# An eight-stage transformer kernel on one core: bias rows added on VectorE, and the memory layer prepared in four blocks

## The reference

```python
x = x + _L0_attn_ref(_layernorm(x), ...)   # 16 heads, softmax
x = x + _L0_ffn_ref(_layernorm(x), ...)    # gelu(x w1 + b1) w2 + b2, 512 hidden
x = x + _L1_attn_ref(_layernorm(x), ...)   # 16 heads of 64
x = x + _L1_ffn_ref(_layernorm(x), ...)
x = x + _L2_attn_ref(_layernorm(x), ...)   # 16 heads over three neighbouring tokens
x = x + _L2_ffn_ref(_layernorm(x), ...)    # 8 experts, the best one
x = x + _L3_attn_ref(_layernorm(x), ...)   # a memory that learns, below
x = x + _L3_ffn_ref(_layernorm(x), ...)    # 8 experts, the best two, and a shared one
```

```python
k, v, q = (causal_dwconv(hidden @ W.T, cw, cb) for k, v, q)          # 4 taps
alpha = (sigmoid(hidden @ aW.T + ab) * 0.1).mean(-1)
eta   = (sigmoid(hidden @ eW.T + eb) * 0.9 + 0.05).mean(-1)
theta = (softplus(hidden @ tW.T + tb) * LR).mean(-1)
# of each chunk: g = clipped gradient of |W2 silu(W1 k) - v|^2 at the chunk's first weights, then
S = eta * S - theta * g ;  W = (1 - alpha) * W + S                  # token by token
out = W2_t silu(W1_t q) ; out = rms_norm(out @ Wo.T) * norm_g * (hidden @ gW.T + gb)
```

## Time and profile before

| what | value |
|---|---|
| time, median of 3 runs | 3157.16 us (3152.45 to 3158.06) |
| profiled execution: its time, its span | 3151.58 us, 3149.8 us |
| PE busy, its weight loads | 2954.1 us (94%), 1838.4 us |
| DVE, ACT, POOL busy | 2210.3, 1419.3, 734.6 us |
| PE clock granted, mean | 0.91 of full speed |

### The profile page before, as it was taken

The page is one execution under the profiler, slowest core; times in us unless marked ns, Lnnn a source line. Parts: engine busy times, 40 slices in busy tenths (PEclk is TensorE's granted clock), DMA queues, the critical chain, the costliest instruction groups (busy, mean ns, idle before and its releaser), DMA issues. The chain is left out here.

```text
span 3149.8 us, 43331 instructions
## 1 busy us (share of the span) xinstructions
PE 2954.1 (94%) x15864; PEld 1838.4 (58%) x15864; DVE 2210.3 (70%) x4583; ACT 1419.3 (45%) x2681; POOL 734.6 (23%) x608
## 2 busy tenths in 40 slices
PE   4999999999987999999999999999999787789799
PEld 2666666666654555555555555555554444556587
DVE  5788888888724877777877777777774637777554
ACT  1666666666641344444444444444444210322343
POOL 1000000000000244444444444444444100055200
PEclk7999999999987899999999999999999867555598
DMA  4112122121004011111111111111100100000000
GB/s 96 26 26 51 29 49 45 33 51 21 1 8 121 1 41 41 41 41 31 38 27 28 41 41 41 41 38 31 35 20 1 37 1 9 3 1 2 16 1 14
DMA packets 42128, 95.91 MB, mean 30 GB/s; under 512 B 12502, under 2 KB 31676, under 8 KB 32188
## 3 DMA queue, kind: packets, MB, share of 16 engines
q1 hardware_dynamic: 41916, 93.14, 13.0%
HBM read 35.18 MB, written 7.34 MB: 13 GB/s over the span
## 5 line engine op out<-in xcount | busy, mean ns | idle before, releaser
L957 ACT ACTIVATE l1a_PT<-l1a_st 128x512 f32<-128x512 f32 x1024 | 597.1, 598 | 759.6 <-PE l1a_st L873 755.5
L974 DVE TENSOR_REDUCE l1a_m<-l1a_aux 128x1 f32<-128x512 f32 x1024 | 667.6, 685 | 125.3 <-PE l1a_aux L835 123.1
L478 DVE TENSOR_REDUCE l0s_mquad<-l0s_mx 128x1 f32<-128x512 f32 x1024 | 635.5, 684 | 169.3 <-PE l0s_mx L346 169.3
L924 POOL TENSOR_TENSOR l1a_acc<-l1a_acc,l1a_PT 128x1024 f32<-128x1024 f32 x224 | 570.0, 2545 | 680.5 <-ACT l1a_PT L957 680.5
L454 ACT ACTIVATE l0s_PT<-l0s_st 128x512 f32<-128x512 f32 x1024 | 529.2, 601 | 236.0 <-PE l0s_st L362 232.6
L886 PE MATMUL l1a_ov<-l1a_PT,l1a_V 128*64 128x512 f32 x2048 | 495.7, 605 | 0.0
L871 PE MATMUL l1a_st<-l1a_QA,l1a_KA 128*128 128x512 f32 x1024 | 447.1, 437 | 2.4 <-issue 2.3
L362 PE MATMUL l0s_st<-l_QS,l_KS 128*128 128x512 f32 x1024 | 437.4, 430 | 3.6 <-ACT l0s_PT L454 3.5
L346 PE MATMUL l0s_mx<-l_KS,l_QS 120*128 120x512 f32 x1024 | 415.9, 412 | 20.4 <-DMA l_KS<-qk_rows 20.4
L873 PE MATMUL l1a_st<-l1a_QB,l1a_KB 65*128 65x512 f32 x1024 | 405.6, 396 | 0.0
L835 PE MATMUL l1a_aux<-l1a_KA,l1a_QA 128*128 128x512 f32 x1024 | 398.5, 437 | 0.8 <-DVE l1a_lo L986 0.8
(11 more groups left out here) (348 smaller groups left out, 2763.7 us busy)
## 6 DMA issues: line engine op xcount, KB each, us to landing
l1a_KA<-l1a_hi SPq DMA_DIRECT2D x32, 512.0 KB, 7.9
l_QS<-qk_rows SPq DMA_DIRECT2D x64, 192.0 KB
l_KS<-qk_rows SPq DMA_DIRECT2D x64, 192.0 KB
l1a_QA<-l1a_hi SPq DMA_DIRECT2D x16, 512.0 KB, 4.5
l1a_QA<-l1a_lo SPq DMA_DIRECT2D x16, 512.0 KB, 8.6
l1a_QB<-l1a_hi SPq DMA_DIRECT2D x16, 512.0 KB, 4.5
l1a_KB<-l1a_lo SPq DMA_DIRECT2D x16, 512.0 KB, 6.4
...
```

What stands on the lines that cost most here:

```text
L478: nc.vector.tensor_reduce(mquad[:, u % 2, tile, g:g + 1], mx[:, n % MX0, :], axis=AX.X, op=ALU.max).then_inc(mx_free[n % MX0], 1)
L924: nc.gpsimd.tensor_tensor(acc[:, h % 2, 1, :], first, PT[:, g % PT_SLOTS, :], ALU.add).then_inc(added_pool, 1)
L957: nc.scalar.activation(PT[:, g % PT_SLOTS, (u % 2) * CW:(u % 2 + 1) * CW], st[:, u % ST1, :], ACT.Exp, scale=1.0 / float(np.sqrt(HD1))).th ...
L974: nc.vector.tensor_reduce(m4[:, b, q, c:c + 1], src, axis=AX.X, op=ALU.max).then_inc(aux_read, 1)
```

## The change

1. The bias rows go. `bv`, `bo`, `b2`, `sb2` and `gb` are loaded as 128 equal rows. In four stages DVE adds the bias to `X` at the stage's start (`add_bias`). V and the gate get it as DVE takes them out of PSUM; for V this moves ACT's copies to DVE, and PE's wait for V is now one for the PSUM buffer (`mx_free`).
2. In `l3_ffn`, the four products of mask and expert biases of a block move from the end into the loop, as one more `down` in groups 7, 9, 11 and 13.
3. `l3_prepare` works in four blocks of 512 tokens. ACT folds tanh, the first tap and abs differently; E runs on 128 partitions (two copies of 32 rows and one of 64), and C and A are one scan beside each other, so that two scans stand for three. The initial values of the multipliers come from POOL, which writes `d1` (128x2048), the zero columns and, later, the squared keys. Key-query products are made two chunks at a time.
4. `l3_scan` scales keys (`ktc`, two ACT operations) and queries (`qa`, two POOL operations) chunk by chunk.
5. Semaphores of early stages are cleared for reuse by POOL at the start of L1's feed-forward.

```diff
+def add_bias(nc, X, bias, biased):
+    for c in range(NC):
+        x = X[:, TPC * c:TPC * (c + 1), :]
+        nc.vector.tensor_tensor(x, x, bias[:, :].unsqueeze(1).broadcast_to([P, TPC, D]), ALU.add).then_inc(biased, 1)
...
-                        nc.tensor.matmul(o[:, t * D:(t + 1) * D], xnT[:, at], Wt[:, 2, :], start=True, stop=False)
-                        last = nc.tensor.matmul(o[:, t * D:(t + 1) * D], ones[0:1, 0:P], bv[0:1, :],
-                                                start=False, stop=True)
+                        last = nc.tensor.matmul(o[:, t * D:(t + 1) * D], xnT[:, at], Wt[:, 2, :], start=True, stop=True)
...
-                nc.tensor.matmul(o, vT[:, t * P:(t + 1) * P], Wo[:, :], start=True, stop=False)
-                nc.tensor.matmul(o, ones[0:1, 0:P], bo[0:1, :], start=False, stop=True).then_inc(done, 1)
+                nc.tensor.matmul(o, vT[:, t * P:(t + 1) * P], Wo[:, :], start=True, stop=True).then_inc(done, 1)
...
+            dve.wait_ge(loaded.sem, loaded.all)
+            add_bias(nc, X, bo, biased)
             for c in range(NC):
+                dve.wait_ge(biased, c + 1)
                 dve.wait_ge(done, TPC * (c + 1))
...
-                        nc.tensor.matmul(o, ones[0:1, 0:P], b2[0:1, :], start=True, stop=False)
                         for b in range(NB):
...
+            if g - 1 in TURNED_AT:
+                mine.append((N3, TURNED_AT.index(g - 1)))
...
-                pe.wait_ge(mt_read, NC)
-                for c in range(NC):
-                    biases(c)
...
+            def sums(c):
+                pe.wait_ge(tanh_done, c + 1)
...
+            project(0)
+            project(1)
+            sums(0)
+            project(2)
+            sums(1)
+            project(3)
+            sums(2)
+            sums(3)
             pe.wait_ge(gain_done, 2)
+            gate(0)
+            gate(1)
+            turn()
             for c in range(NC):
+                key_query(c)
+            gate(2)
+            gate(3)
...
+            def conv(c):
+                dve.wait_ge(raw_done, c + 1)
+                dve.wait_ge(y_done, c + 1)
...
+                nc.vector.tensor_tensor_scan(T["E"][:, cols(c)], eta[:, cols(c)], d1[:, cols(c)], 0.0, ALU.mult, ALU.add
+                                             ).then_inc(e_done, 1)
+                dve.wait_ge(e_done, c + 1)
+                nc.vector.tensor_tensor_scan(T["C"][:, cols(c)], oma[:, cols(c)], T["E"][:, cols(c)], 0.0,
+                                             ALU.mult, ALU.add).then_inc(c_done, 1)
...
-                    nc.tensor.matmul(y1, state[:, o % 4, 0, 0, :], T["qA"][:, at(o)], start=True, stop=False)
+                    nc.tensor.matmul(y1, state[:, o % 4, 0, 0, :], qa[:, o % 2, 0, :], start=True, stop=False)
...
+                    for i, th in enumerate((thC, thE)):
+                        nc.scalar.activation(ktc[:, c % 2, i, :], T["ktok"][:, c, :], ACT.Copy, scale=th[:, c:c + 1]
+                                             ).then_inc(s["ktc_done"], 1)
...
+                    for i, coef in enumerate((T["A"], T["C"])):
+                        nc.gpsimd.tensor_tensor(qa[:, c % 2, i, :], T["q"][:, at(c)], coef[0:DM, at(c)], ALU.mult
+                                                ).then_inc(s["qa_done"], 1)
...
-            for kt, th in ((ktokC, thC), (ktokE, thE)):
-                link.open(nc.vector.tensor_tensor(kt[:, :, :], T["ktok"][:, :, :],
-                                                  th[:, :].unsqueeze(2).broadcast_to([CHUNK, NCH, DM]), ALU.mult))
```

More of the change, by code:

```diff
@@ L1780, in _ @@
                     add(d, *downs[d])
-                for c in range(NC):
-                    add(len(downs) + c, N3, c)
 DM = 32
@@ new lines, in gate, with turn @@
+            def gate(i):
+                b = GATE_BANK[i]
+                pe.wait_ge(oma_done, 2 * (b + 1))
+                if b == 0:
+                    pe.wait_ge(kt_read, 2)
+                for t in range(TPC):
+                    n = TPC * i + t
+                    last = nc.tensor.matmul(pp[:, b, t * D:(t + 1) * D], xnT[:, n * P:(n + 1) * P], gW[:, :],
+                                            start=True, stop=True)
+                last.then_inc(gate_full, 1)
+            def turn():
+                pe.wait_ge(conv_done, NC)
+                for n in range(NT):
+                    last = nc.tensor.transpose(pp[:, 0, n * DM:(n + 1) * DM], T["k"][0:DM, n * P:(n + 1) * P],
+                                               ident[0:DM, 0:DM])
+                last.then_inc(kt_full, 1)
@@ new lines, in key_query @@
+            def key_query(c):
+                pe.wait_ge(eta_done, 2 * (c + 1))
+                pe.wait_ge(q_done, c + 1)
+                for n in range(TPC * c, TPC * (c + 1)):
+                    at = slice(n * P, (n + 1) * P)
+                    last = nc.tensor.matmul(pb[:, c, (n % TPC) * P:(n % TPC + 1) * P], T["k"][0:DM, at], T["q"][:, at],
+                                            start=True, stop=True)
+                last.then_inc(kq_full, 1)
+            project(0)
+            project(1)
@@ L1934, in _ @@
+            gate(2)
+            gate(3)
+            pe.wait_ge(ln_done, 1)
+            pe.wait_ge(gate_read, 1)
+            for n in range(NT):
+                last = nc.tensor.matmul(pp[:, 1, n:n + 1], soft[MAIN, n * P:(n + 1) * P], lead[MAIN, 1:2],
+                                        start=True, stop=True)
+            last.then_inc(th_full, 1)
         @block.scalar
         def _(act):
-            link = Chain(act, act_order)
             act.wait_ge(loaded.sem, loaded.all)
-            link(nc.scalar.activation(raw[:, 0:TAPS - 1], cw[:, 0:TAPS - 1], ACT.Copy, scale=0.0))
@@ new lines, in _ @@
+            project(0)
+            project(1)
+            act.wait_ge(d1_set, 1)
+            eta_of(0)
+            project(2)
+            eta_of(1)
+            project(3)
+            eta_of(2)
+            eta_of(3)
+            for c in range(NC - 1):
+                query(c)
+            move(0)
+            for c in range(NC - 1):
+                value(c)
+            query(NC - 1)
+            act.wait_ge(half_set, 1)
+            act.wait_ge(abs_done, NC)
+            nc.scalar.activation(soft[3 * DM:4 * DM, :], tn[low, :], ACT.Ln, scale=0.5, bias=half[low, :]).then_inc(ln_done, 1)
@@ new lines, in _ @@
+            dve.wait_ge(raw_set, 1)
+            conv(0)
+            conv(1)
+            dve.wait_ge(starts_set, 2)
+            dve.wait_ge(d1_set, 1)
+            scans(0)
+            conv(2)
+            scans(1)
+            conv(3)
+            scans(2)
+            dve.wait_ge(gain_done, 2)
+            gate(0)
+            scans(3)
+            gate(1)
+            for c in range(NC):
+                key_query(c)
+            gate(2)
+            gate(3)
+            dve.wait_ge(ksq_done, 1)
```

438 lines of the change are left out of this document (219 added, 219 removed).

## The result

The changed kernel takes 3076.82 us (median of 4 runs, 3072.86 to 3079.14) against 3154.80 (median of 4, 3147.02 to 3158.06); the ratio is 0.9755, 95% interval 0.9732 to 0.9778. It is 78 us faster; the forecast of 3072 was 4.8 us too low.

What follows compares the result with a forecast made beforehand. PE was taken to bound most attention and feed-forward stages, DVE `l3_prepare`, a ring of small steps the scan. Terms summed to -81.9 us: 3069.7 from the profiled execution, 3075.3 from the median, forecast 3072; 8-in-10 range 3057 to 3091.

Steps and rivals of the forecast that it cites:

- Surcharge of height: PE, alternating product heights: each product costs about 0.27 us (slow clock) or 0.19 (fast) more; removing bias products returns it.
- L0 attention and output: V products and output projection of L0 without bias products: -10.7 us and -10.3 us.
- L0 feed-forward: L0's feed-forward, PE-bound: 16 tiles at -0.63 us each without bias products, -10.1 us.
- L2 attention: L2's output projection: four blocks, each dropping from 5.79 to 1.79 us on the path, -16.0 us.
- Last feed-forward: End of the last feed-forward: -11.4 us at the end, +5.1 for mask products returning in four groups, -6.3 us.
- Preparation: `l3_prepare`, bound by DVE: 32.6 us of work, 4.3 of waits including 1.6 for theta's products; -32.3 us.
- Scan's start: Start of the L3 scan: two DVE operations go and ACT's table load comes ahead, -2.3 us.
- Scan: L3 scan: DVE operations starting right after POOL ones lengthen, 0.19 us per chunk for 31 chunks, +5.8 us.
- Only the bias product's own time goes: Rival, bias stages: remaining tall products stay at 0.72 or 0.40 us, together 15.7 us dearer, 3088; 12%.
- Blocks don't overlap: Rival, `l3_prepare`: each block's chain runs alone, so -10 us instead of -32, 3094; 6%.
- POOL blocks DVE: Rival, scan: DVE waits until a running POOL operation ends, 0.5 us per chunk, +16 instead of +5.8, 3082; 10%.
- Cheaper than forecast: Rival: no lengthening hit in the scan (-5.8 us) and bias products hidden as laid out, 3062 to 3066; 10%.

Runs made afterwards that it cites:

- the second repetition: The changed kernel itself, unaltered, measured and profiled again as the measure for other runs: 3074.23 us (5 runs), ratio 0.9753.
- the run of all three together: Changed kernel with key-query products of blocks 0 and 1 before second gate block, queries scaled by POOL over all tokens, keys squared after last scan: 3070.45 us, repeated 3066.74.
- The run with early products: Changed kernel with key-query products of blocks 0 and 1 put ahead of the second gate block on PE: 3074.91 us, ratio 0.9742.
- the full-height run: Kernel before, all bias products kept, but those of L0's V, output, feed-forward and L2's output contract over 128 partitions: 3118.23 us, ratio 0.9904.

## Why the prediction was right, and where not

It was right in direction and within its range, and by its own mechanisms but for the end of the preparation and the price in the scan:

- **Surcharge of height.** Right, and shown. 0.447 and 0.218 for the products left over were 0.43 to 0.47 and 0.22. The Trainium skill ("TensorE: Matmul & The Clock Gate", Step-by-step) says that the number of rows doesn't matter to a weight load. The spacing of the products agrees among 96, 127 and 128 rows, but not where 1 to 64 stand beside 128; the measurement decides.
- **L0 attention and output**: -21.0, measured -21.8 (12.0 up to the output, forecast 10.7; 9.8 in it, forecast 10.3). The 1.3 us more lie ahead of the output and have no run of their own; the clock is at 1.00 through the rounds from 68.0 us on, before from 78.8. The layout of the output names "3.3 - 1.26" for its end, but its 907.8 comes out with 3.3 - 1.95. What I had set at nothing, a late transfer of the bias in the output projection, is there, with 1.4 us.
- **L0 feed-forward**: per period -2.45 us, forecast -2.5; the stage's other 2 us lie before the first tile and go with the clock, which rises 4 us into the stage instead of 10. The stage takes 37.7 to 37.9 us in all three profiles of the changed kernel against 49.4 and 49.8, but 40.9 and 41.3 in two other runs with the same code.
- **L2 attention**: 3.9 us per block, forecast 4.0. The stage's -13.0 has 2.2 us of a later clock in it; the second repetition shows 106.13 - 90.95 = -15.2.
- **Last feed-forward**: -6.3, measured -6.5. The insertion cost 4.4, not 5.1.
- **Preparation**: -32.3, measured -27.5. The step that failed is the end of the layout: "1.6 for theta's products" is 5.1. The 16 products load weights of 128 columns and take 7.0 us, 0.44 each at the slow clock; the 32 of the kernel before (L1906) loaded 64 columns and took 6.98 us together, 0.22 each. I priced the new ones like the old ones: 16 x 0.22 = 3.5 us are what the 1.6 lacks to 5.1. The Trainium skill ("TensorE: Matmul & The Clock Gate", Step-by-step) says that a load's time goes with its columns; the trace agrees, 0.44 against 0.22, though the rows differ too (64 against 32). The lock on the last scan cost DVE 1.7 us more, which vanish in that wait (the run of all three together). The run with early products shows that PE, not DVE, ends this stage.
- **Scan's start**: -2.3, measured -2.3 (from the preparation's last operation on DVE to the first chunk's mark 6.0 us, before 8.3).
- **Scan**: +5.8, measured +5.0 (5.52 against 5.36, 31 gaps). The size was right for the wrong reason, which is luck. I took 0.09 us for a toll on starts that meet, and held the lock for a rival of +16. The lock is what there is; its price is only what POOL's 0.31 us still has to run when DVE's operation would end, two times 0.09.
- **Rivals.** "Only the bias product's own time goes" fell (the full-height run). "Blocks don't overlap" fell: DVE has no wait on record from its first convolution at 2650.19 to the last key-query scaling at 2682.22. "POOL blocks DVE" was right as a mechanism and wrong in its price. "Cheaper than forecast" fell, as the hold in the scan is there. "Slower than before" was never near: POOL still idles 0.35 us before `h2a` in most chunks, 0.3 in the forecast.
- **The total.** Between -82.2 and -72.7 lie 9.5 us: 4.8 in the preparation; 4.3 in L2's feed-forward (2 to 5 in all ten profiles with the changed code ahead of it), which no step of the prediction had, since it took stages with the same work as the same length; 2.7 + 2.2 of a later clock in L1's feed-forward and L2 attention, which are this execution's. The other way go 1.5 in L1 attention, this execution's too, and 2.0 in L0's feed-forward, which all three profiles of the changed kernel have. The rest is 0.8 or less for each term. The medians are 78.0 us apart.
